# A two-layer decoder on one core: the last expert layer computed for each token's own experts, in sorted tiles, instead of densely

## The reference, cut to what matters

```
probs = softmax(x @ w_router)                       # 1024 tokens, 16 experts
top_w, top_i = top_k(probs, 4);  top_w /= sum(top_w)
g   = silu(x @ we1[e]) * (x @ we3[e])               # all e, width 128
moe = sum over the 4 chosen e of top_w * (g @ we2[e])
shared = (silu(x @ ws1) * (x @ ws3)) @ ws2          # width 512
x = layernorm(x + shared / 5 + moe * 4 / 5)
```

## Time and profile before

| | |
|---|---|
| median of 3 runs | 902.44 us (900.88 to 908.67) |
| the profiled execution | 903.48 us |
| its span in the trace | 901.7 us |
| PE busy | 801.8 us, 89% of the span |
| DVE, ACT, POOL busy | 574.4, 429.2, 499.8 us |
| last piece loop begins, last sum of it ends | 720.9 us, 893.3 us |

### The profile page before, as it was taken

The page is one execution under the profiler, slowest core; times in us unless marked ns, Lnnn a source line. Parts: engine busy times, 40 slices in busy tenths (PEclk is TensorE's granted clock), DMA queues, the critical chain, the costliest instruction groups (busy, mean ns, idle before and its releaser), DMA issues. The chain is left out here.

```text
span 901.7 us, 14551 instructions
## 1 busy us (share of the span) xinstructions
PE 801.8 (89%) x4733; PEld 685.0 (76%) x4733; DVE 574.4 (64%) x1651; ACT 429.2 (48%) x1209; POOL 499.8 (55%) x411
## 2 busy tenths in 40 slices
PE   7899999999999876792789999998987599999995
PEld 5678888888888764490678888887875388888885
DVE  4696867868769466123677667876736655545545
ACT  4264635536446544162366665666663532232232
POOL 4757287556587351513455564556422367777774
PEclk8999999999999997896999999999999799999998
DMA  6220711212315112553001111011001011111111
GB/s 200 71 94 1 234 36 59 94 36 106 115 50 180 55 54 65 186 120 88 30 6 48 53 53 53 1 54 53 24 1 37 12 35 52 35 52 52 35 41 47
DMA packets 58331, 59.09 MB, mean 66 GB/s; under 512 B 5392, under 2 KB 49312, under 8 KB 58272
## 3 DMA queue, kind: packets, MB, share of 16 engines
q1 hardware_dynamic: 57504, 56.24, 20.0%
q0 software_dynamic: 768, 2.10, 0.7%
HBM read 50.00 MB, written 8.32 MB: 65 GB/s over the span
## 5 line engine op out<-in xcount | busy, mean ns | idle before, releaser
L889 ACT ACTIVATE a_probs<-bank,a_neg_peak 128x128 f32<-128x128 f32 (+1 forms) x256 | 103.2, 429 | 88.9 <-DVE a_neg_peak L997 88.9
L917 ACT ACTIVATE a_probs<-a_probs,a_row_inv 128x128 f32<-128x128 f32 (+1 forms) x256 | 92.0, 447 | 20.8 <-DVE a_row_inv L1005 20.7
L997 DVE CUSTOM_DVE_ANT_0 bank<-bank,causal 128x128 f32<-128x128 f32 (+1 forms) x256 | 82.3, 394 | 15.3 <-PE bank L759 15.3
L895 ACT ACTIVATE a_probs_t<-bank 128x512 f32<-128x512 f32 x96 | 53.9, 597 | 73.5 <-PE bank L779 73.5
L1700 POOL TENSOR_TENSOR d_h_lo<-d_h,d_h_hi 128x512 fp32r<-128x512 f32 x40 | 51.7, 1293 | 52.6 <-ACT d_h_hi L1819 39.0
L398 POOL TENSOR_TENSOR a_wk_hi<-raw_k,one 128x512 fp32r<-128x512 f32 (+1 forms) x24 | 21.6, 901 | 102.3 <-DMA raw_k<-in_L_attn_w_k_dram 64.1
L798 PE MATMUL bank<-a_probs_t,a_vals 128*128 128x256 f32 x256 | 76.5, 380 | 0.0
L118 PE MATMUL bank<-a_wo_hi,a_ot_hi 128*128 128x256 f32 x256 | 74.5, 291 | 0.7 <-DVE a_ot_lo L1017 0.7
L1905 DVE TENSOR_TENSOR d_h<-d_silu,bank 128x512 f32<-128x512 f32 x40 | 27.5, 688 | 72.9 <-PE bank L120 72.8
L119 PE MATMUL bank<-a_wo_lo,a_ot_hi 128*128 128x256 f32 x256 | 73.2, 286 | 0.0
L120 PE MATMUL bank<-a_wo_hi,a_ot_lo 128*128 128x256 f32 x256 | 73.1, 286 | 0.0
(11 more groups left out here) (316 smaller groups left out, 2429.5 us busy)
## 6 DMA issues: line engine op xcount, KB each, us to landing
d_raw<-in_L_ffn_we_dram SPq DMA_DIRECT2D x48, 128.0 KB, 2.2
raw_k<-in_L_attn_w_k_dram SPq DMA_DIRECT2D x8, 512.0 KB, 6.5
raw_q<-in_L_attn_w_q_dram SPq DMA_DIRECT2D x8, 512.0 KB, 5.7
raw_v<-in_L_attn_w_v_dram SPq DMA_DIRECT2D x8, 512.0 KB, 7.3
raw_o<-in_L_attn_w_o_dram SPq DMA_DIRECT2D x8, 512.0 KB, 3.7
kv<-_L_ffn_expert_masks_dram SPq DMA_DIRECT2D x16, 256.0 KB, 3.1
kvt<-_L_ffn_expert_masks_dram SPq DMA_DIRECT2D x16, 256.0 KB, 3.1
raw_q<-in_L_attn_Wq_dram SPq DMA_DIRECT2D x8, 512.0 KB, 4.7
```

The costliest lines, as they stand in the source:

```text
L889: nc.scalar.activation(probs[s % 2][:, i, at:at + width], c.banks[i][:, at:at + width], ACT.Exp, bias=neg_peak[:, n:n + 1], scale=-1.0, ac ...
L895: nc.scalar.activation(probs_t[:, i * BANK:(i + 1) * BANK], c.banks[3 + (3 * s + i) % 2][:], ACT.Copy).then_inc(s_pt_free, 1)
L917: last = nc.scalar.activation(part, part, ACT.Copy, scale=row_inv[:, s % 2, n + r:n + r + 1])
L997: last = nc.vector.tensor_tensor_reduce(part, part, mask, -1.0, 3e38, ALU.add, ALU.min, neg_peak[:, n + r:n + r + 1])
```

## The change

- The router works half by half of the tokens (`choose`, `find`, `gates`). `find` gives each token four places, one for each of its experts, in a list sorted by expert, each expert's part rounded up to tiles of 128 rows. A half has 31 tiles, in 16 pairs.
- The zeros for the two sorted lists (`c.sorted1`, 4096 rows of 1 KB each) are written in the attention of layer 1, by one 2 MB DMA in each of SP's groups 1 to 4.
- All weights stay in SBUF. The first 8 pieces (of 20) have their low part made by GpSimd, the other 12 by VectorE, the high parts all by ScalarE.
- The shared expert runs densely, in 8 steps (4 slices by 2 halves). The 16 experts run over the 32 pairs of sorted tiles: `turn` (transposes), `hidden`, `turn_hidden` (transposes), `outputs`. Weights are addressed through registers.
- GpSimd scatters `x` with 32 indirect DMAs, and later gathers results with 32: the first 16 after the first half's results are stored, the last 16 after the second half's. VectorE adds four gathered rows per token, times their gates (`combine`).
- To make room, some tiles are freed before this block, and semaphores of earlier blocks are cleared and used again.

```diff
@@ decoder
+        c.sorted1 = [nc.dram_tensor(f"sorted_rows1_{half}", (2 * PAIRS1 * P, D), F32, kind="Internal").ap() for half in range(2)]
@@ attention, SP's list
                     if not rope and g == 2:
                         blank = c.idle[:].bitcast(F32).unsqueeze(1).broadcast_to([P, CHUNKS * BANK // P, D])
                         sp.dma_start(c.sorted_rows.rearrange("(t p) d -> p t d", p=P), blank).then_inc(c.s_blank, 16)
+                    if rope and g <= 4:
+                        blank = c.idle[:].bitcast(F32).unsqueeze(1).broadcast_to([P, PAIRS1, D])
+                        rows = slice((g - 1) % 2 * PAIRS1 * P, ((g - 1) % 2 + 1) * PAIRS1 * P)
+                        sp.dma_start(c.sorted1[(g - 1) // 2][rows].rearrange("(t p) d -> p t d", p=P), blank).then_inc(c.s_blank, 16)
...
@@ cross_and_experts, GpSimd
+                def scatter(half):
+                    pool.wait_ge(s_place, half + 1)
+                    for t in HALF_TILES[half]:
+                        for k in range(TOPK):
+                            nc.gpsimd.indirect_dma_start(c.sorted1[half], bass.IndirectOffsetOnAxis(place[:, t, k:k + 1], 0), c.x[:, t], None).then_inc(s_scattered[half], 16)
+                def gather(t):
+                    if t % (NT // 2) == 0:
+                        for i in range(4):
+                            pool.wait_ge(s_stored[i], 16 * (PAIRS1 // 4) * (t // (NT // 2) + 1))
+                    if t >= 2:
+                        pool.wait_ge(s_summed, t - 1)
+                    for k in range(TOPK):
+                        nc.gpsimd.indirect_dma_start(got[t % 2][:, k], None, y_sorted[t // (NT // 2)], bass.IndirectOffsetOnAxis(place[:, t, k:k + 1], 0)).then_inc(s_got[t % 2], 16)
...
@@ TensorE
-                up(0, 0)
-                pe.wait_ge(s_above, 1)
-                with pe.Fori(0, PIECES // 2 - 1) as i:
-                    up(i, 1)
-                    down(i, 0)
-                    up(i + 1, 0)
-                    down(i, 1)
...
+                for n in range(1, STEPS1):
+                    if n + 1 < STEPS1:
+                        up(n + 1)
+                    down(n)
+                turn(0)
+                turn(1)
+                split_wait(pe, len(Pieces.ORDER) - 1)
+                columns = {}
+                for i in range(ALL + 2):
+                    if i < ALL:
+                        if i % 4 == 0:
+                            columns[i // 4] = columns_of(i)
+                        hidden(i, columns[i // 4])
+                    if 1 <= i <= ALL:
+                        turn_hidden(i - 1)
+                    if i + 2 < ALL:
+                        turn(i + 2)
+                    if i >= 2:
+                        outputs(i - 2, columns[(i - 2) // 4])
...
@@ ScalarE
+                for n in range(STEPS1):
+                    shared(n)
+                    high(n + 8)
+                    shared_high(n)
+                for n in pieces.by_dve[STEPS1:]:
+                    high(n)
+                for half in range(2):
+                    act.wait_ge(s_above, half + 1)
+                    nc.scalar.activation(likely[:, part_of(half)], above[:, part_of(half)], ACT.Exp).then_inc(s_likely, 1)
+                nc.scalar.activation(primed[:], c.one[:], ACT.Silu)
+                sorted_high(0)
+                sorted_high(1)
...
@@ VectorE
+                for n in pieces.by_dve[STEPS1:]:
+                    low(n)
+                shared_total(1)
+                sorted_low(0)
+                sorted_low(1)
+                AT = {PAIRS1 + 5 + 2 * j: j for j in range(NT // 2)}
+                for i in range(ALL + 1):
+                    if i < ALL:
+                        gated(i)
+                    if i >= 1:
+                        hidden_low(i - 1)
+                    if i + 2 < ALL:
+                        sorted_low(i + 2)
+                    if i in (2, 4):
+                        gates(i // 2 - 1)
+                    if i in AT:
+                        combine(AT[i])
+                aggregate(0)
+                norm6.apply(dve, 0, s_norm6)
+                for t in HALF_TILES[1]:
+                    combine(t)
+                aggregate(1)
+                norm6.apply(dve, 1, s_norm6)
```

More of the change, by code:

```diff
@@ L1718, in _ @@
[L1718 to L1721 removed]
+                pool.wait_ge(s_norm5, NT)
+                for n in range(5, 8):
+                    low(n)
+                pool.wait_ge(c.s_blank, 16 * 5)
+                scatter(0)
+                scatter(1)
+                for t in HALF_TILES[0]:
+                    gather(t)
+                norm6.root(pool, 0)
+                for t in HALF_TILES[1]:
+                    gather(t)
@@ new lines, in columns_of @@
+                def columns_of(i):
+                    if i % PAIRS1 == 0:
+                        pe.wait_ge(s_column, i // PAIRS1 + 1)
+                    first = i % PAIRS1 // 4 * 8
+                    _, columns = nc.values_load_multi_w_load_instructions(column[i // PAIRS1][0:1, first:first + 8], engines=[mybir.EngineType.PE], min_val=0, max_val=(EXPERTS1 - 1) * 2 * PIECE,
+                                                                          skip_runtime_bounds_check_because="VectorE counts at least 0 experts and takes at most the last")
+                    return columns
@@ new lines, in _ @@
+                turned5.dve(dve, halves=[0])
+                norm5.apply(dve, 1, s_norm5)
+                choose(0)
+                turned5.dve(dve, halves=[1])
+                find(0)
+                shared(0)
+                shared_low(0)
+                choose(1)
+                shared(1)
+                shared_low(1)
+                find(1)
+                LOWS_AT = {2: (8,), 3: (9, 10), 4: (11,), 5: (12, 13), 6: (14,), 7: (15,)}
+                for n in range(2, STEPS1):
+                    shared(n)
+                    for m in LOWS_AT[n]:
+                        low(m)
+                    shared_low(n)
+                    if n == SHARED:
+                        shared_total(0)
```

678 lines of the change are left out of this document (454 added, 224 removed).

## The result

The changed kernel took **950.16 us** (median of 4 runs, 944.60 to 958.72) where the kernel before took 903.91 beside it: a ratio of 1.0515, 95% interval 1.0417 to 1.0612. The direction was as forecast, the size was not: 5.2% slower instead of 1.7%, 33 us above the 917.5, and 19 above the range.

A forecast was written before the change was run, and what follows sets the result against it. TensorE's issue was taken to bound the last stage, and weight landing layer 1's attention. Span 901.7 + 24.6 lost - 7.6 gained = 918.7, rounded to 917, plus 0.7, gave 917.5 us (range 894 to 931).

The forecast's parts named there:

- Zeros, the mechanism: Layer 1 attention: zeros queued on SP ahead of raw_q and raw_k delay TensorE's scores; this part loses 24.6 us.
- Rivals 1 and 2: First: zeros delay nothing, 895 us, chance 0.2. Second: 16 us lost and 14 gained, 905 us, chance 0.2.
- Zeros, the wait: Layer 1 attention, groups 1 to 3: each 2 MB of zeros adds 5.7 us, with no slack, 17.1 us.
- Zeros, the clock: Layer 1 attention: TensorE's low clock after idling costs 2 us for each of three stalls, 6 us.
- Zeros, group 4: Layer 1 attention, group 4: 4.2 us of slack before TensorE needs the queries, so at most 1.5 us lost.
- the bound of 28: Upper bound on the loss from zeros in layer 1's attention: 3 x 6.1 + 4 + 6 = 28 us.
- The early stage: Last block, router and shared steps: 46 us after 720.9, including 7 us from down(7)'s end to the first hidden.
- The sorted loop: Last block's sorted experts: 31 steps of 2.77 us, 86 us, plus 5 us for ends and low clock.
- Rival 3: Register-address issue, or VectorE and GpSimd's shared port, bounds loop or scatters: 3.3 us a step, 934 us, chance 0.1.
- The tail: From the last matmul to the end: 36.1 us, including 16 gathers at 20.4 us and 1.1 us for contention.
- The sum: Whole kernel: 24.6 us lost, 7.6 us gained, span 918.7 rounded down to 917, time 917.5 us.
- each is asked for at least one step after what it needs: Sorted loop: ScalarE's 1.8 us and VectorE's 1.5 us a step fit within TensorE's 2.77 us.

The follow-up runs named there:

- zeros_alone: Kernel before with only the four 2 MB DMAs of zeros added, ahead of raw_q and raw_k in layer 1: 932.47 us, ratio 1.0327.
- zeros_warm: Kernel before with the four 2 MB zeros DMAs, plus 28 idle matmuls on TensorE ahead of the scores in three groups: 930.07 us, ratio 1.0295.
- after_again: The changed kernel, unaltered, run again on another chip: 927.13 us, ratio 1.026 to the kernel before.
- Best: Changed kernel with zeros issued after GpSimd's first split, the shared steps' end reordered and the first half's bn_aggr inside the loop: 929.89 us, ratio 1.0251.
- best_2: The same reordered version of the changed kernel as Best, run once more on another chip: 928.85 us.
- After_third: The changed kernel, unaltered, run on a third chip: 965.28 us, ratio 1.0648 to the kernel before.
- late_scatters_2: Changed kernel with zeros after GpSimd's first split and the 32 scatters only after the shared steps' last down, on a chip with late signals: 950.57 us.
- plain_scatters_2: Changed kernel with zeros after GpSimd's first split and scatters replaced by plain DMAs on SP, on a chip with late signals: 919.42 us.
- plain_scatters: Changed kernel with zeros after GpSimd's first split and scatters replaced by plain DMAs on SP, on a chip without late signals: 907.21 us.

## Why the prediction was wrong, point by point

- **Zeros, the mechanism**: right. "Nothing lies between the landing of the weights and TensorE" held: three groups with 7.3, 7.1 and 7.9 us idle, a clock of 0.50 behind, and moving the DMAs gives it back. Rivals 1 and 2 fall.
- **Zeros, the wait** ("I take 5.7"): mis-sized, and nearly all of what this part missed. In groups 1 to 3 it comes to 21.5 us instead of 17.1. 2 MB added 6.7 to 7.7 us in the changed kernel and 6.1 to 7.2 alone; 1 MB added 3.1 to 3.9. The 9.2 us for 3 MB in layer 0 gave too little for one MB, 3.1 where it is 3.3 to 3.5 here; why was not tried.
- **Zeros, the clock** ("2 us for each of three stalls"): right. The three groups of the changed kernel grew by 9.3, 9.0 and 9.7 us and their waits by 7.2, 6.7 and 7.7, so 2.0 to 2.3 a stall are left; zeros_alone leaves 2.3 to 2.7, and zeros_warm nothing where the stall is covered.
- **Zeros, group 4** ("at most 1.5"): 2.2 to 2.7. The slack was as read (4.1 us, forecast 4.2); the wait grew by 6.2 to 6.7 where 5.7 was taken. Sum of the part 30 to 31 us instead of 24.6, above the bound of 28.
- **The early stage** ("begins at 720.9 + 46", so 86.8 us after the block's start): 87.4 to 89.1 in the undisturbed profiles in which nothing there was altered, 87.8 in after_again. "7 us between the end of down(7) and the first hidden" were 6.6 to 7.7. Right, where nothing disturbs it; 92.5 in the first profile. The 1.28 us a table load stand in it twice, at 803.52 and 805.24, each with the next activation 0.02 us behind its end. The Trainium skill (ScalarE: Activation LUTs, What ACT_TABLE_LOAD costs) states 2.66 us with the drain; this trace has the load's part of it, 1.28 us, and no drain behind.
- **The sorted loop** ("2.77 a step", 91 us with its ends): 2.82 a step, 91.1 us. Rival 3's register addresses cost nothing that shows. 100.2 in the first profile.
- **The tail** (36.1): 37.5. The term that I left out is the first half's root ahead of gather 4, with 4.08 us between its two instructions: the first gather came 5.3 us after the last matmul instead of 4.0. Best and best_2, with the root inside the loop, have 3.5 and a tail of 35.5 and 35.3. The gathers in the loop started 1.25 us apart while VectorE combined, so the allowance of 1.1 us for contention was not needed. The block that I had taken from the Trainium skill (SBUF — State Buffer, Who interferes with whom) did not show there; the same section says that an instruction like `combine` takes only the shared read side while the making of descriptors needs the write side, which it marks as inferred, and the 1.25 us agree with that.
- **The sum**: without late signals the program takes 927.1 us. Of its span of 925.8, which is 8.8 above the 917 of the forecast, 4.6 are in the block's start (709.45 against 680.25 + 24.6), 2.5 in the last stage and 1.7 were rounded away ("I round the two parts' doubts down", an argument that no run bears out). 927.1 is inside the range, in part by luck: the zeros cost 30.3 us there, 5.7 more than forecast, and 3.0 of it were hidden because this execution happened to be that much earlier at its first `raw_o` of layer 1 (468.7 against 471.7).
- **What failed** is the step "each is asked for at least one step after what it needs", and its like in the shared steps: it put the way of a signal from TensorE to the next engine at nothing, without a reason. In the first profile that failed under the scatters (4.7 us) and the gathers (9.1 us). Against after_again's span of 925.8 these 13.8 us and 6.2 at the block's start make the 945.7; 5.7 of the 6.2 were there at the first `raw_o` of layer 1 (474.4 against 468.7), ahead of all zeros, in the spread of stages that no kernel altered (467.9 to 474.9 over 20 profiles). After_third lost 34 us to the late signals, 23 in the shared steps and 11 in the loop. No rival had this. Rival 3 (register addresses, or the port of VectorE and GpSimd) also put something on the loop or the scatters, at 16 us, but neither of its causes shows: the undisturbed steps were 2.82 us long.
- **Slips in the working**, none of which moves the forecast by more than 0.2 us: 917 + 0.7 is 917.7 and not 917.5; from 477.16 to 480.78 are 3.62 us and not 3.65; and "TensorE's work falls by over 80 us" does not follow from its own terms, since 16 pieces of 8.48 us less 31 steps of 18 x 0.115 us give 72, and 53 with the transposes.

The kernel before has scatters and gathers too, in its masked experts, but TensorE waits for them there and has nothing to signal.

## What to carry to other kernels

A DMA that nobody waits for is still a wait for whoever loads behind it: queue it after the loads, at a time when the queue is otherwise empty, which took 27.8 us off the changed kernel (927.1 to 899.3 on one chip). Price a stall with the clock behind it, 2.0 to 2.7 us on top of the 7 us idle here. And before GpSimd's indirect DMAs are put beside a stage that hands work between TensorE and the others every few us, time it on several chips: 927, 950 and 965 us were the same program.

## What the hardware showed that I had not expected

- TensorE's signals to ScalarE and VectorE come late by its own records, up to 6.1 us in the first profile, 14.7 in late_scatters_2's and 24.9 in best's, and leave TensorE idle for 13 to 22 us in the later profiles, under GpSimd's indirect DMAs and only on some chips; the kernel before stays at 902 to 906 us on all of them.
- Between the two instructions of GpSimd's root (a `TENSOR_SCALAR` of 0.20 and a `pow` of 1.04 us) lie 4.08 us the first time behind the scatters and gathers, and 1.47 the second; it was 0.15 ahead of any in this block (717.61 to 717.96). In plain_scatters, with gathers and no scatters, it was 1.47 the first time too and the tail 35.4 us long, so the gathers alone do not make the 4.08.
- A piece of 393 KB that could be copied 4.8 us after its load was issued took 7.0 with 1 MB of sorted rows ahead of it.
